# Late stage of an attention-and-experts kernel: four early up products instead of two, and one fixed order for the rest of the up products and the turned probabilities

## What is computed

```python
x = x + attention(layernorm(x), ctx)
xt = layernorm(x).reshape(2048, 512)
probs = softmax of the two largest of 7 router logits, else 0     # per token
u = xt @ Wup[e] + bup[e]
g = silu(u @ Wgate[e] + bgate[e]) * u
eo = g @ Wdown[e] + bdown[e]
out = sum_e probs[:, e] * eo[e]
su = xt @ Wsu + bsu;  sg = silu(su @ Wsg + bsg) * su;  so = sg @ Wsd + bsd
x = x + out + so
```

## Time and profile before

| what | value |
|---|---|
| median of three runs | 993.65 us |
| the profiled execution, its own time | 995.3 us |
| its span, first to last instruction | 993.6 us |
| mean granted TensorE clock (1 is full speed) | 0.962 |
| TensorE matmuls busy | 909.5 us |
| VectorE busy | 636.0 us |
| ScalarE busy | 459.5 us |
| GpSimd busy | 563.9 us |

### The profile page before, as it was taken

One profiled execution on the slowest core, in us unless ns is written; L12 is line 12 of the kernel. 1 busy time (PEld: TensorE's weight loads), 2 busy tenths in 40 slices (PEclk: granted clock), 3 DMA queues, 4 the chain that ended last, 5 costly groups with the idle time before them and its releaser, 6 DMA issues. The chain is left out here.

```text
span 993.6 us, 16827 instructions
## 1 busy us (share of the span) xinstructions
PE 909.5 (92%) x5047; PEld 406.6 (41%) x5048; DVE 636.0 (64%) x1019; ACT 459.5 (46%) x846; POOL 563.9 (57%) x487
## 2 busy tenths in 40 slices
PE   3889895799999999989999689999999999999898
PEld 1345442122221222246644245555555555555443
DVE  7888777588787988467776144554554444443388
ACT  3375665678877888722353022332233233323540
POOL 5465556367777775543127499989999920000372
PEclk9798998599999999999999799999999999999999
DMA  7234635445454532133425766666566643335676
GB/s 233 77 92 122 179 105 166 139 158 169 167 177 159 177 105 70 53 107 128 153 112 218 289 191 209 217 200 220 201 215 205 201 139 106 121 109 187 232 203 221
DMA packets 106059, 162.26 MB, mean 163 GB/s; under 512 B 12536, under 2 KB 55608, under 8 KB 105616
## 3 DMA queue, kind: packets, MB, share of 16 engines
q1 hardware_dynamic: 92768, 115.86, 35.9%
q0 software_dynamic: 12896, 45.10, 13.6%
q10 hardware_dynamic: 336, 0.57, 0.2%
HBM read 107.88 MB, written 53.48 MB: 162 GB/s over the span
## 5 line engine op out<-in xcount | busy, mean ns | idle before, releaser
L1089 ACT ACTIVATE p_t<-a_psT 128x512 f32<-128x512 f32 x256 | 138.9, 595 | 47.4 <-PE a_psT L1212 46.1
L1136 DVE TENSOR_REDUCE nm<-quad 128x4 bf16<-128x1984 f32 x60 | 133.9, 2231 | 35.7 <-PE quad L1197 35.7
L1905 ACT ACTIVATE e_xT<-quad 128x512 f16<-128x512 f32 x38 | 22.7, 597 | 229.9 <-PE quad L1969 229.9
L1979 PE MATMUL quad<-w_exp,e_xT 128*128 x456 | 107.2, 386 | 4.9 <-DVE e_xT L1933 2.6
L1039 POOL TENSOR_TENSOR p_sum<-p_t,p_t 128x512 f32<-128x512 f32 x64 | 81.1, 1275 | 53.2 <-ACT p_t L1089 53.0
L1979 PE MATMUL quad<-w_exp,e_uT 128*128 x456 | 104.6, 379 | 0.0
L1979 PE MATMUL e_psY<-w_exp,e_gT 128*128 x456 | 104.6, 379 | 0.0
L1212 PE MATMUL a_psT<-q_stk,k_stk 98*128 98x512 f16 x256 | 84.6, 401 | 11.2 <-ACT p_t L1089 9.4
L215 POOL TENSOR_TENSOR w_exp<-e_raw,w_exp 128x1024 f16<-128x1024 f32 x42 | 91.7, 2184 | 3.5
L1936 DVE SCALAR_TENSOR_TENSOR e_g<-quad,bias 128x512 f32<-128x512 f32 x38 | 26.3, 691 | 85.4 <-PE e_psGT L1969 80.5
L1936 DVE SCALAR_TENSOR_TENSOR e_u<-quad,bias 128x512 f32<-128x512 f32 x38 | 26.3, 691 | 73.9 <-PE quad L1979 73.9
(11 more groups left out here) (338 smaller groups left out, 1797.0 us busy)
## 6 DMA issues: line engine op xcount, KB each, us to landing
xs_dram<-zero SPq DMA_DIRECT2D x38, 256.0 KB, 6.9
bias<-in_L_ffn_bup_dram SPq DMA_DIRECT2D x38, 256.0 KB, 3.3
bias<-in_L_ffn_bgate_dram SPq DMA_DIRECT2D x38, 256.0 KB, 3.4
ys_dram<-e_y SPq DMA_DIRECT2D x38, 256.0 KB, 2.0
e_x<-xs_dram SPq DMA_DIRECT2D x36, 256.0 KB, 2.8
q_dram<-q_st SPq DMA_DIRECT2D x24, 256.0 KB, 3.0
k_dram<-k_st SPq DMA_DIRECT2D x24, 256.0 KB, 3.6
q_stk<-q_dram SPq DMA_DIRECT2D x64, 96.0 KB
```

The lines of the kernel that those rows point to most:

```text
L1089: act.activation(probs(w, k), psT[:, k % 2], ACT.Exp, scale=SCALE / (QS * QS)).then_inc(s["exp"], 1)
L1136: dve.tensor_reduce(nm[:, i, :, 0:1].rearrange("p h o -> p (h o)"), psS[:, :, 0:NMAIN], AX.X, ALU.max, negate=True)
L1979: ins = pe.matmul(dst[:, :], stationary, moving, start=(k == 0), stop=(k == len(terms) - 1))
```

## The change

`UP_EARLY` goes from 2 to 4. The first early up chunk stays where it was. The second no longer stands between the down products of blocks 36 and 37: chunks 1, 2 and 3 stand behind the last down product, in psU, psUT and psG, with two waits ahead of them on copies and sums of the last block. In the late stage TensorE then has no up chunk of group 0 left and makes all four of group 1 first, then `turn_probs(0)` and `(1)`; `turn_probs(2)` and `(3)` go behind the first and the second gate chunk of group 0. ScalarE has the same order: four `up(0, c)`, the two copies of the biases, four `up(1, c)`, `turned_probs(0)` and `(1)`, and `turned_probs(2)` and `(3)` behind the first two gates. The programs of VectorE, GpSimd and SyncE are the same as before.

```diff
-UP_EARLY = 2
+UP_EARLY = 4
...
                     pe.wait_ge(late_ld, 32)
                     pe.wait_ge(g_["split_done"], (E + 1) * (2 * NM) + 2 * NM + 1)
                     pe.wait_ge(s["xT_l"], N)
-                if isinstance(n, int) and N <= n < N + UP_EARLY:
-                    late_up(n - N, (psX, psU)[n - N])
+                    late_up(0, psX)
+                if isinstance(n, int) and n == N + 2:
+                    pe.wait_ge(s["uT_l"], N)
+                    pe.wait_ge(s["g_in"], N)
+                    for c in range(1, UP_EARLY):
+                        late_up(c, (psX, psU, psUT, psG)[c])
...
-            up(0, 0)
-            up(0, 1)
-            up(0, 2)
+            for c in range(KD):
+                up(0, c)
             act.wait_ge(s["d_loaded"], 16 * 6)
             act.activation(bd_hi[:, :], bd_raw[:, :], ACT.Copy, scale=WS).then_inc(s["bd0"], 1)
             act.activation(bd_16[:, :], bd_raw[:, :], ACT.Copy, scale=WS).then_inc(s["bd0"], 1)
-            up(0, 3)
+            for c in range(KD):
+                up(1, c)
             turned_probs(0)
             turned_probs(1)
-            up(1, 0)
-            up(1, 1)
-            turned_probs(2)
-            turned_probs(3)
-            up(1, 2)
-            up(1, 3)
             for grp in range(GRP):
                 for c in range(KD):
                     gate(grp, c)
+                    if grp == 0 and c < 2:
+                        turned_probs(2 + c)
                     if c:
                         gated_hi(grp, c - 1)
                 gated_hi(grp, KD - 1)
...
             for c in range(UP_EARLY, KD):
                 up(0, c)
+            for c in range(KD):
+                up(1, c)
             turn_probs(0)
             turn_probs(1)
-            up(1, 0)
-            up(1, 1)
-            turn_probs(2)
-            turn_probs(3)
-            up(1, 2)
-            up(1, 3)
             for c in range(KD):
                 gate(0, c)
+                if c < 2:
+                    turn_probs(2 + c)
                 if c >= 2:
                     first_bias(c - 2)
```

## The result

Over 14 runs each, on the same chips, the changed kernel has a median of 998.36 us (995.51 to 1002.3) and the kernel before 994.72 us (992.55 to 998.34): a ratio of 1.0034, 95% interval 1.0021 to 1.0046. So the change costs 3.4 us, with 95% certainty between 2.1 and 4.6, where +2.8 was forecast.

The account below looks back on a forecast made before the run. TensorE was taken to bound the late stage, with VectorE already level at first_bias(2). The later first_bias(2), 1.1, plus slow clock, 1.7, gave +2.8 us: 996.4 against a median of 993.65, range 993.0 to 998.9.

Parts of the forecast that it names:

- The border: Border into the late stage: TensorE, not SyncE, comes last; the new stage starts 3.2 us later, hole shrinks to 0.3.
- TensorE's own order: Behind the border, with 24 matmuls less, TensorE waits 0.3 us at turn_probs(2) and reaches first_bias(2) at 957.3, free at 957.4.
- VectorE's order: Gathered tiles up to first_total(0): later gathers end it at 962.1, first_bias(2) comes 1.1 us later, TensorE idles 4.7.
- The clock: TensorE behind the new hole at first_bias(2): low clock costs 1.7 us, bounds nothing to 1.85.
- The price of before: First 24 late-stage matmuls of the kernel before: slow clock behind the 3.17 us hole was said to cost 1.85 us.
- the faster rival: At first_bias(2): VectorE keeps up and TensorE never waits; -4.0 us, 989.6; chance 0.10.
- The reason given: At first_bias(2): gathers starting 3.2 us later cause a 4.7 us wait that takes back more than all that was won.
- the wait without a slow clock: At first_bias(2): the 4.7 us hole comes but little runs at the low clock; +1.1 us, 994.8; chance 0.17.
- The slower one: VectorE's tiles 2 and 3: gathers lose more than 3.2 us; tile 2 2.5 later gives +5.3, 998.9; chance 0.15.
- The contention with GpSimd: Late stage: two-input VectorE instructions in SBUF contend with GpSimd instructions reading it; pointed to the slower rival, no size given.

Follow-up runs that it names:

- The filled hole: Changed kernel plus 22 matmuls of no use ahead of first_bias(2); ratio 1.0030 to the kernel before.
- first gathers early: Changed kernel, but GpSimd issues the gathers of tiles 0 and 1 ahead of the border, at its routed program's end; ratio 1.0055 to the kernel before.
- two chunks behind: Changed kernel with UP_EARLY = 3: chunks 1 and 2 behind the last down product, chunk 3 behind the border; ratio 1.0012 to the kernel before.
- border part alone: Changed kernel with the late stage's old order on TensorE and ScalarE; chunks 1 to 3 stay behind the last down product; ratio 1.0032 to the kernel before.
- totals early: Changed kernel with VectorE's first_total(0) to (3) each two chunks earlier; ratio 0.9985 to the kernel before.

## Why the prediction was right

It forecast +2.8 and 996.4 us against a median of 993.65; with the 14 runs of both the shift is +3.4 (2.1 to 4.6). The mechanism came as forecast: a border 3.2 later, a wait for the gathers, a hole of 4 to 5 us at first_bias(2), the clock. The size was a little short. The median of 998.36 lies inside the stated range but above the forecast's own (995.6 to 997.7); 1.1 of the difference from 996.4 is that the median of before, too, came out at 994.72 with more runs. And two errors partly cancel: first_bias(2) was put 1.1 later and came 1.9 later on the way, while the clock was put at 1.7 and cost 1.4. By its steps:

- **The border.** 3.2 later by the forecast, 3.38 measured. The wait for psY was put at 0.7 and is 0.88: the copy ended at 914.80 and the product began at 915.04, a gap of 0.24 that was not reckoned in full. TensorE comes last at the border, as said, and the hole is 0.32 for 0.3.
- **TensorE's own order.** The wait at turn_probs(2) was put at 0.3 and is 0.42. TensorE comes to first_bias(2) 28.8 behind the border (959.83 - 5.11 - 925.89), forecast 28.6 (957.4 - 928.8).
- **VectorE's order.** This is the term that was mis-sized. The pair of tile 2 was there 16.2 behind the border (forecast 16.6). From there to the end of first_total(0) it took 17.7 (959.78 - 942.06), forecast 16.7: 16.1 of work and 0.6 of waiting. The wait at tile 4 was 1.09 (bounds 0.3 to 0.9), since tile 2 had come earlier, and "the later tiles come at its own pace" was wrong: VectorE waited for tile 5 as well, until 950.57. The reason is in GpSimd's rows. Its issues for tiles 4 and 5 took 1.34, 1.21, 1.14 and 0.95, together 4.64 us, where they had taken 3.88 before; from issue to landing it took 3.6 to 3.7, before 3.2 to 3.6. Why the issues took longer no run shows. In sum first_total(0) ended 33.9 behind the border, forecast 33.3, and the hole is 5.11 for 4.7.

```profile
942.29 1.34 POOL L2133 DMA_INDIRECT l_rows_back<-ys_dram,slot  x1 [1.03 <-DMA l_rows_back<-ys_dram,slot]
943.93 1.21 POOL L2133 DMA_INDIRECT l_rows_back<-ys_dram,slot  x1 [0.30 <-issue]
```

- **The clock.** 1.7 forecast, 1.4 measured; it fell just ahead of the end of the hole (0.97 over the 5.1 us of it), and 0.55 was granted for the 3.4 us behind it. The filled hole showed the cause, in the profile. The price of before was misread: 7.03 in place of 5.18, which gave 1.85, compares a time that has the modelled end in it with one that has not (24 matmuls at full clock show as 5.34). The next instruction starts 6.87 behind the first of them (932.51 - 925.64), so 1.69 was lost. That touches the upper bound and the faster rival, not the 1.7.
- **The reason given.** "The gathers start 3.2 later" is borne out by the step from three chunks to two, where the end follows the border one to one, and by the early gathers, which made the part behind the border 2.9 shorter. As the price of a later border in general it is too narrow, though: with the old order a hole of 4.19 stands at ScalarE's copy of the turned probabilities instead.

The Trainium skill, TensorE: Matmul & The Clock Gate, section HAM oscillation, has it that matmuls behind a wait in mid-stream run at half rate, at a penalty of half of the throttled time. The traces agree: before, 3.4 us low cost 1.69; in the changed kernel 3.4 us low cost 1.42, a part of the low stretch lying ahead of the first matmul.

Of the rivals, the wait without a slow clock fell to the profile, the faster one to the hole of 5.11. The slower one did not come by itself, since the first gathers landed in 7.5 to 7.9 and the second ones in 3.6 to 4.7; but holding the loads back made a kernel of that sort, +6.16 on the way, with a gather of 7.3 and VectorE waiting for it, at tile 5 and not at tile 2. The contention with GpSimd that was named beside this rival is not shown: VectorE's two sums per tile took 1.53 to 1.54 us in both kernels, and for the longer issues at tiles 4 and 5 no run separates a cause.

## What to carry to other kernels

Early work behind a stage's last product was free here as long as it ended before the slowest engine reached the border. From there on each microsecond of it delays every other engine's start, and if one of those starts a chain that the busy engine later waits for, it comes back whole. So fill the hole at a border and no more: here one chunk of 2.6 us won 3.2 (in the old order, half of it by the clock that stayed), two won nothing and three lost 3.4. And an in-order engine that sums things up for others should do first what someone waits for, which here took a hole of 5.11 us down to two of 1.5 together.

## What was not expected of the hardware

- GpSimd's drain is long: it ended 3.5 us beyond the last instruction with no gather in flight (before), and 4.5 beyond the last issue with gathers in flight (first gathers early). So work that GpSimd does just ahead of a border can push it back by more than its own length, as it did there.
- A hole of 3.16 (two chunks behind), of 4.19 (border part alone) and of 5.11 (changed) was followed by a low clock each time, 0.55 or 0.56 for 3.4 us, while two waits of 1.11 and 0.40 (totals early) were not.
- Executions of the same code ahead of the late stage differ by some 3 us and more (the down product of block 36 starts at 911.41, 914.54 or 916.98), which is as much as the whole effect. Only a way measured from a common point within the trace showed effects of half a microsecond.
